# The norm inside the layers, applied by GpSimd instead of ScalarE, in a macaron block of attention, experts and a recurrence

## The chip, the cores and the metric

One core of a Trainium2 chip runs the whole kernel. The metric is the time of one execution on the device, in microseconds. The kernel before took 5356.07 us in the median of three runs (5350.53, 5356.07, 5367.39).

## The reference, cut to what matters

The input is a batch of 8 sequences of 512 tokens with 128 features. Six blocks follow each other; the change touches the second, a stack of six layers:

```
for l in range(LAYERS):                      # 6
    keys = concatenate([past, x])            # past: one row of zeros
    q, k, v = x @ Wq.T + bq, keys @ Wk.T + bk, keys @ Wv.T + bv     # 16 heads of 8
    scores = q @ k.T / sqrt(8), only keys at 0 to 125 places before the query
    o = softmax(scores) @ v;  o = o @ Wo[l].T + bo[l]
    x = _ln(x + o, ln1_g[l], ln1_b[l])       # norm of kind 1
    ff = gelu(x @ W1[l].T + b1[l]) @ W2[l].T + b2[l]
    x = _ln(x + ff, ln2_g[l], ln2_b[l])      # norm of kind 2
# _ln(x, g, b) = (x - mean) * rsqrt(var + 1e-5) * g + b, over the 128 features
```

Ahead of the layers stands a block of routed experts, behind them another one, then causal attention with a mixture of experts, a recurrence over time, and attention with experts again.

## The kernel before, in words

The activations of all tokens lie in `A`, 32 tiles of 128 tokens x 128 features, four tiles to a sequence. Each engine has its own program of the layers; they are tied together by semaphores, and each engine works strictly in the order in which its program is written.

**Stages, units, items.** A stage is one sequence in one layer: 6 x 8 = 48 stages. A stage is two units (r = 0 and 1), each with half of the heads, and a unit is four items (i = 0 to 3), one for each block of 128 keys. An item has two halves. In each half TensorE runs a `bracket`: scores of an item five ahead (`S`, L1251, read by VectorE for the row minima, L2197), and the turned scores of this item (`T`, L1266), which ScalarE turns into probabilities (L1832). GpSimd then masks the probabilities of an item by two `affine_select` (L945, L950), and TensorE multiplies them by the values (`values`, L1306) two items later: the values of item 0 stand in the program at item 2. The result banks are two rings: D, four banks that VectorE frees (`l_d_ev`), and A, three banks that ScalarE frees (`l_a_ev`).

**What runs beside it.** Projections of the next stage, the transposes and the feed-forward of earlier stages are put between the brackets (`shared`, `feed_forward`): in stage s, the projection of the heads' output of stage s - 1, the feed-forward's up part of stage s - 2 (L1227, six and two matmuls) and its down part of stage s - 3 (L1237). The norm of kind 1 of stage s - 2 belongs to unit 0 of stage s, the norm of kind 2 of stage s - 3 to unit 1. After the 48 stages three more empty out the pipeline, in which there is no attention.

**The norm.** VectorE adds the branch to `A` and takes mean and variance of each token (L2130, L2134) into `mv`, and signals `l_var_ready`. The rest was split over two engines:
- GpSimd, `root` (L954): at the start of a unit, ahead of the select of item 0, it takes the root of the variance by three Newton steps on 128 x 4 numbers (`newton_rows`, L910 to L928, each step linked to the one before by a semaphore), then multiplies the mean by it (L960) and negates the product (L961), into `r1`, and signals `l_rstd_ready`.
- ScalarE, `apply` (L1846): in the second item, after the exponentials of its first half, it waits for that signal, and for each of the four tiles computes `A * rstd + r1` in place (L1850), then signals `l_applied`. In its program the copy of the head sums (`sums`, L1844) and the exponentials of the item's second half come next.
- GpSimd, `affine` (L963): after the select of item 1 it waits for `l_applied` and multiplies by g (L970) and adds b (L971) over all four tiles, and signals the turned rows of the next step (`attn_out`, `ffn_out`). The results of kind 1 are wanted in unit 1 of the same stage, those of kind 2 by the next layer.

`chain.link` waits for the instruction that it issues, `chain.add` only counts it, and `chain.join` waits for all that were counted.

Of the kernel before, what the change touches and what calls it, by code (L numbers as in the profile page):

```python
# [20 lines left out]
ALU = mybir.AluOpType  # L21
ACT = mybir.ActivationFunctionType
# [3 lines left out]
BATCHES, TOKENS = 8, 512  # L26
TPB = TOKENS // P
# [25 lines left out]
class Tally:  # L53


    def __init__(self):
        self.base, self.n = 0, 0
# [110 lines left out]
class LayerPipeline:  # L168
# [9 lines left out]
    def __init__(self, sem):  # L178
        both = (0, 1)
        self.scored = [ScoreItem(0, both, 0, KPAD + P, True)] + \  # L180
            [ScoreItem(i, both, KPAD + P * (i - 1), 2 * P) for i in range(1, TPB)]
        self.turned = [TurnedItem(j, both, P * j, min(2 * P, TOKENS - P * j)) for j in range(TPB)]
        self.d_done, self.d_ev = sem("l_d_done"), sem("l_d_ev")
        self.a_done, self.a_ev = sem("l_a_done"), sem("l_a_ev")
        self.mask_done = sem("l_mask_done")
        self.pv_done = sem("l_pv_done")
        self.od_ev = sem("l_od_ev")
        self.pad_ready = sem("l_pad_ready")
        self.rows_ready = sem("l_rows_ready")
        self.var_ready = sem("l_var_ready")  # L190
        self.rstd_ready = sem("l_rstd_ready")
        self.applied = sem("l_applied")
        self.D, self.A, self.norm = {}, {}, {}
        self.number(("D", "prep", 0))
        for use in self.first_projections():
            self.number(use)
        for m in range(self.LEAD):
            for g in range(4):
                self.number(("D", "S", m, g))
        self.number(("D", "max0", 0))  # L200
        for u in range(self.UNITS + 5):
            for i in range(self.ITEMS):
                for half in range(2):
                    for use in self.bracket(u, i, half) + self.shared(u, i, half):
                        self.number(use)
            if u % 2:
                for use in self.feed_forward(u // 2):
                    self.number(use)
        for s in range(self.STAGES + 2):
            if 0 <= s - 1 < self.STAGES:  # L210
                self.norm[1, s - 1] = len(self.norm)
            if 0 <= s - 2 < self.STAGES:
                self.norm[2, s - 2] = len(self.norm)
# [217 lines left out]
def build(nc, d, out):  # L431
    ctx = ExitStack()
    with ctx:
        def sb(name, shape, dt=F32):
            return ctx.enter_context(nc.sbuf_tensor(name, shape, dt))
# [47 lines left out]
        r1 = sb("r1", [P, TILES])  # L483
        r2 = sb("r2", [P, TILES])
        stats = sb("stats", [P, TILES, 6])
        mv = sb("mv", [P, TILES, 2])
        rstd = sb("rstd", [P, TILES])
# [6 lines left out]
        at = [0]  # L494

        def take(*shape):
            n = int(np.prod(shape))
            v = arena[:, at[0]:at[0] + n]
            at[0] += n
            assert at[0] <= 34048  # L500
            if len(shape) == 2:
                v = v.rearrange("p (a b) -> p a b", b=shape[1])
            if len(shape) == 3:
                v = v.rearrange("p (a b c) -> p a b c", b=shape[1], c=shape[2])
            return v


        A = take(TILES, P)
# [115 lines left out]
        L = LayerPipeline(sem)  # L624
# [218 lines left out]
        def _(pool):  # L843
            chain = Chain(pool, g_chain)
# [44 lines left out]
            m = mask_win0[:, 1:2]  # L889
# [12 lines left out]
            m = mask_win0[:, KPAD:]  # L902
# [34 lines left out]
            def layers():  # L937

                def select(m):
                    t = L.turned[m % L.ITEMS]  # L940
                    view = PTs[m % L.SLOTS][:, 0:8 * t.w].rearrange("p (h q) -> p h q", q=t.w)

                    pool.wait_ge(L.a_ev, L.A["T", m, 3] + 1)
                    a = view[:, :, 0:P]
                    pool.affine_select(out=a, in_=a, compare_op=ALU.is_ge, fill=0.0, base=0,  # L945
                                       pattern=[[0, 8], [1, P]], channel_multiplier=-1).then_inc(L.mask_done, 1)

                    pool.wait_ge(L.mask_done, 2 * m + 1)
                    a = view[:, :, PAST + 1:t.w]
                    pool.affine_select(out=a, in_=a, compare_op=ALU.is_ge, fill=0.0, base=-1,  # L950
                                       pattern=[[0, 8], [-1, t.w - PAST - 1]], channel_multiplier=1)\
                        .then_inc(L.mask_done, 1)

                def root(kind, s):  # L954
                    at = TPB * (s % BATCHES)
                    n = L.norm[kind, s]
                    nb = r1[:, at:at + TPB]
                    pool.wait_ge(L.var_ready, n + 1)
                    chain.link(newton_rows(TPB, at))
                    chain.link(pool.tensor_tensor(nb, mv[:, at:at + TPB, 0], rstd[:, at:at + TPB], ALU.mult))  # L960
                    pool.tensor_scalar(nb, nb, -1.0, None, ALU.mult).then_inc(L.rstd_ready, 1)  # L961

                def affine(kind, s):  # L963
                    l, b = divmod(s, BATCHES)
                    x = A[:, TPB * b:TPB * (b + 1), :]
                    rows, g = (arows[l % 2], 2) if kind == 1 else (frows[l % 2], 1)
                    pool.wait_ge(L.applied, L.norm[kind, s] + 1)

                    pool.wait_ge(L.rows_ready, 2 * l + 1 if kind == 1 else min(2 * l + 2, 2 * LAYERS - 1))
                    chain.link(pool.tensor_tensor(x, x, row(rows[:, g, :]), ALU.mult))  # L970
                    pool.tensor_tensor(x, x, row(rows[:, g + 1, :]), ALU.add)\  # L971
                        .then_inc(attn_out if kind == 1 else ffn_out, 1)

                for s in range(L.STAGES + 3):
                    for r in range(2):
                        kind, b = (1, s - 2) if r == 0 else (2, s - 3)
                        normed = 0 <= b < L.STAGES
                        if normed:
                            root(kind, b)
                        for i in range(L.ITEMS):  # L980
                            if s < L.STAGES:
                                select(L.ITEMS * (2 * s + r) + i)
                            if i == 1 and normed:
                                affine(kind, b)
                            enter(0, s, r, i)
# [790 lines left out]
        def _(act):  # L1776
            chain = Chain(act, a_chain)
# [3 lines left out]
            def layers():  # L1781
# [61 lines left out]
                        act.wait_ge(L.d_done, L.D["od", u - 1] + 1)  # L1843
                    act.activation(ODs[0], ps[:, L.SUMS, :], copy).then_inc(L.od_ev, 1)  # L1844

                def apply(kind, s):  # L1846
                    act.wait_ge(L.rstd_ready, L.norm[kind, s] + 1)
                    for i in range(TPB):
                        t = TPB * (s % BATCHES) + i
                        m = act.activation(A[:, t, :], A[:, t, :], ACT.Identity, bias=r1[:, t:t + 1],  # L1850
                                           scale=rstd[:, t:t + 1])
                    m.then_inc(L.applied, 1)

                def shared(u, i, half):
                    for ring, name, n, *r in L.shared(u, i, half):
                        if ring == "D":
# [20 lines left out]
                for u in range(L.UNITS + 6):  # L1877
                    s, r = divmod(u, 2)
                    for i in range(L.ITEMS):
                        for half in range(2):  # L1880
                            if (i, half) == (1, 1) and 0 < u <= L.UNITS:
                                sums(u - 1)
                            if u < L.UNITS:
                                for k in (2 * half, 2 * half + 1):
                                    probs(L.ITEMS * u + i, k)
                            shared(u, i, half)
                            if (i, half) == (0, 1) and u + 1 < L.UNITS:
                                pad_probs(u + 1)
                            if (i, half) == (1, 0):
                                kind, b = (1, s - 2) if r == 0 else (2, s - 3)  # L1890
                                if 0 <= b < L.STAGES:
                                    apply(kind, b)
                    if r:
                        for ring, name, n, *c in L.feed_forward(s):
                            if ring == "A":
                                hidden(n, *c)
# [211 lines left out]
            for b in range(2, BATCHES):  # L2108
                act.wait_ge(R.y_done, b + 1)
                for i in range(TPB):  # L2110
                    t = TPB * b + i
                    m = act.activation(A[:, t, :], ps[:, 4 + b % 4, i * P:(i + 1) * P], ACT.Identity,
                                       bias=zero[:, 0:1], scale=rstd[:, t:t + 1])
# [708 lines left out]
```

## Time and profile before

| | |
|---|---|
| median of 3 runs | 5356.07 us |
| profiled execution, its own time | 5366.25 us |
| its span | 5364.5 us |
| TensorE busy (matmuls) | 4340.6 us, 81% |
| VectorE busy | 3354.4 us, 63% |
| ScalarE busy | 2537.7 us, 47% |
| GpSimd busy | 1798.7 us, 34% |
| mean granted clock of TensorE | 0.877 |
| ScalarE's applies (L1850) | 384 in the layers, 484 ns each |

The busy shares are means over blocks with different limits. The layers run from about 295 to 2420 us; of what follows, the change touches nothing. In the profile PE is TensorE's matmuls and PEld its weight loads, DVE is VectorE, ACT is ScalarE and POOL is GpSimd; L1850 is line 1850 of the kernel. A row with "x4" merges four instructions of one line that follow each other, with the time from the first's start to the last's end. What stands in brackets is the idle time of the engine ahead of the instruction, and what ended it. `arena` is the large buffer that holds nearly all tiles.

### The profile page before, as it was taken

How to read it: one execution, taken by the hardware profiler on the slowest of the kernel's cores; microseconds unless marked ns; L12 is line 12 of the kernel's file. 1: busy time of each engine (PE TensorE's matmuls, PEld its weight loads, DVE VectorE, ACT ScalarE, POOL GpSimd, SP SyncE). 2: the span in 40 equal slices, each digit the busy share in tenths (PEclk: the TensorE clock that was granted, in tenths of full speed). 3: DMA queues.
4: the chain of work that ended last, by engine and by line, in shares of the span. 5: the costliest groups of instructions: out<-in, count | busy, mean ns of one | idle time of the engine just before them, and what ended most of it. 6: DMA issues, size and time to landing. Idle time of an engine off the chain costs nothing.

```text
span 5364.5 us, 114679 instructions
## 1 busy us (share of the span) xinstructions
PE 4340.6 (81%) x42902; PEld 2557.6 (48%) x42902; DVE 3354.4 (63%) x15572; ACT 2537.7 (47%) x4908; POOL 1798.7 (34%) x3712
## 2 busy tenths in 40 slices
PE   2789999999999999972689999657470069999999
PEld 2645555555555555542643446435340034446777
DVE  2187777777777777732156752699999957772111
ACT  1346777777777777741334544333230024553333
POOL 3155666666666666653123220000000022220000
PEclk9879999999999999985878989778685558998999
DMA  4500000000000000002401000010000000000000
GB/s 125 153 10 2 2 12 2 6 8 2 12 2 6 8 2 6 2 1 79 142 5 39 1 1 13 13 25 16 16 17 16 0 11 1 1 1 3 5 5 7
DMA packets 131690, 104.40 MB, mean 19 GB/s; under 512 B 22048, under 2 KB 110400, under 8 KB 131136
## 3 DMA queue, kind: packets, MB, share of 16 engines
q1 hardware_dynamic: 127040, 88.67, 6.1%
q0 software_dynamic: 4096, 8.40, 0.5%
q8 instruction: 341, 5.59, 0.4%
q14 instruction: 213, 1.74, 0.1%
HBM read 74.56 MB, written 22.48 MB: 18 GB/s over the span
## 4 chain that ended last, share of the span: by engine, by line
PE 58%; DVE 21%; ACT 7%; POOL 7%; issue 6%; SPq 1%; DMA 1%; POOLq 0%; DVEq 0%; ACTq 0%
PE ps L1676 6%; PE ps L1668 6%; PE ps L1266 5%; PE ps L1306 5%; PE ps L1451 4%; PE ps L1251 4%; PE ps L1463 4%; PE ps L1227 3%; PE ps L1237 3%; PE ps L1492 2%; DVE arena L2697 2%; DVE arena L2717 2%; PE ps L1136 2%; ACT arena L1850 2%; ACT arena L1832 2%
## 5 line engine op out<-in xcount | busy, mean ns | idle before, releaser
L2197 DVE CUSTOM_DVE_ANT_0 arena<-ps,mask_win 128x256 f32<-128x256 f32 (+1 forms) x3072 | 1008.6, 385 | 257.1 <-PE ps L1251 255.1
L1832 ACT ACTIVATE arena<-ps 128x512 f32<-128x512 f32 (+1 forms) x1536 | 751.5, 543 | 562.6 <-PE ps L1266 553.9
L1266 PE MATMUL ps<-arena 32*64 32x384 f32 (+2 forms) x6144 | 742.9, 478 | 72.6 <-ACT arena L1832 72.2
L1676 PEld LDWEIGHTS ps<-w,arena 128*128 128x128 f32 x4096 | 546.8, 196 | 356.9 <-issue 282.1
L1251 PE MATMUL ps<-arena 32*64 32x192 f32 (+2 forms) x12288 | 694.6, 323 | 14.7 <-DVE arena L2197 14.1
L1676 PE MATMUL ps<-w,arena 128*128 128x128 f32 x4096 | 554.5, 279 | 115.5 <-ACT arena L2086 63.1
L2086 ACT ACTIVATE arena<-ps,eb 128x512 f32<-128x512 f32 x512 | 351.1, 687 | 621.6 <-PE ps L1668 621.4
L2370 DVE CUSTOM_DVE_ANT_0 arena<-ps,mask_cau 128x512 f32<-128x512 f32 (+3 forms) x1024 | 446.4, 486 | 272.7 <-PE ps L1451 270.2
L1949 ACT ACTIVATE arena<-ps 128x512 f32<-128x512 f32 (+2 forms) x768 | 363.0, 526 | 482.9 <-PE ps L1463 482.8
L945 POOL TENSOR_SCALAR_AFFINE_SELECT arena<-arena 128x1024 f32<-128x1024 f32 x384 | 419.8, 1093 | 394.2 <-ACT arena L1832 391.4
L1668 PE MATMUL ps<-arena,w 128*128 128x512 f32 x1024 | 537.0, 608 | 0.0
L1463 PE MATMUL ps<-arena 32*128 32x512 f32 (+2 forms) x1536 | 503.0, 643 | 24.2 <-ACT arena L1949 24.0
L1251 PEld LDWEIGHTS ps<-arena 32*64 32x64 f32 x12288 | 379.9, 133 | 270.5 <-DVE arena L2197 96.0
L1451 PE MATMUL ps<-arena 32*128 32x512 f32 (+3 forms) x2048 | 437.3, 529 | 22.4 <-DVE arena L2370 17.1
L2598 DVE SCALAR_TENSOR_TENSOR X<-ps,C,X 128x128 f32<-128x128 f32 x512 | 143.7, 343 | 469.0 <-PE ps L1676 468.9
L1306 PE MATMUL ps<-arena 128*32 128x256 f32 (+1 forms) x6144 | 387.4, 371 | 14.1 <-POOL arena L950 14.1
L997 POOL TENSOR_SCALAR_AFFINE_SELECT arena<-arena 128x512 f32<-128x512 f32 (+1 forms) x192 | 153.6, 801 | 727.8 <-ACT arena L1949 727.2
L1136 PE MATMUL ps<-ident,arena 128*128 128x128 f32 x912 | 170.2, 318 | 271.4 <-DMA arena<-xs 120.5
L950 POOL TENSOR_SCALAR_AFFINE_SELECT arena<-arena 128x1040 f32<-128x1040 f32 (+1 forms) x384 | 341.8, 890 | 26.2
L910 POOL TENSOR_SCALAR nv<-mv 128x4 f32<-128x4 f32 (+3 forms) x136 | 32.1, 236 | 855.5 <-DVE mv L2134 850.9
L1451 PEld LDWEIGHTS ps<-arena 32*128 32x128 f32 x2048 | 198.1, 212 | 190.6 <-issue 90.2
L1266 PEld LDWEIGHTS ps<-arena 32*64 32x64 f32 x6144 | 217.5, 132 | 149.5 <-ACT arena L1832 145.8
(315 smaller groups left out, 7683.4 us busy)
## 6 DMA issues: line engine op xcount, KB each, us to landing
w<-in_L_w_dram SPq DMA_DIRECT2D x160, 256.0 KB
arena<-xs SPq DMA_DIRECT2D x10, 512.0 KB, 6.8
ys<-arena SPq DMA_DIRECT2D x10, 512.0 KB, 4.4
xs<-zero SPq DMA_DIRECT2D x1, 2560.0 KB, 11.2
w<-in_L_w_dram SPq DMA_DIRECT2D x1, 2048.0 KB
scr_k<-arena SPq DMA_DIRECT2D x8, 256.0 KB, 2.3
scr_v<-arena SPq DMA_DIRECT2D x8, 256.0 KB, 2.8
scr_f<-arena SPq DMA_DIRECT2D x8, 256.0 KB, 3.2
```

The source lines that it names most:

```text
L945: pool.affine_select(out=a, in_=a, compare_op=ALU.is_ge, fill=0.0, base=0, pattern=[[0, 8], [1, P]], channel_multiplier=-1).then_inc(L.mas ...
L1251: m = pe.matmul(ps[64 * h:64 * h + 64, bank, s.at(v) + lo:s.at(v) + hi], Q[p][r][rows, v, q0:q0 + 64], K[p][r][rows, s.k0 + lo:s.k0 + hi], ...
L1266: m = pe.matmul(out[64 * h:64 * h + 64, :, lo:hi], K[p][r][rows, t.k0 + lo:t.k0 + lo + 64], Q[p][r][rows, 0:2, t.q0 + lo:t.q0 + hi], start ...
L1306: x = pe.matmul(ps[32 * g:32 * g + 32, L.SUMS, t.q0:t.q0 + t.w], Vx[p][:, t.block, at:at + 32], PTs[m % L.SLOTS][:, (2 * k + v) * t.w:(2 * ...
L1451: m = pe.matmul(ps[:, g, s.at(v):s.at(v) + s.kw], Q[p][r][rows, v, s.tile * P:(s.tile + 1) * P], K[p][r][rows, s.k0:s.k0 + s.kw], start=Tr ...
L1463: pe.matmul(ps[:, 4 + k % 2, 0:w].rearrange("p (v q) -> p v q", q=t.w), K[p][r][rows, t.k0:t.k0 + P], Q[p][r][rows, t.vs[0]:t.vs[-1] + 1, ...
L1668: pe.matmul(out if use else out.rearrange("p (i t) -> p i t", t=P), E1(e)[:, c * P:(c + 1) * P], rows(g), start=True, stop=True).then_inc( ...
L1676: m = pe.matmul(ps[:, 2 + e % 2, i * P:(i + 1) * P], hid[c % 2][:, i * P:(i + 1) * P], E2(e)[:, c, :], start=(c == 0 and i == 0), stop=(c ...
L1832: act.activation(PTs[m % L.SLOTS][:, k * w:(k + 1) * w], bank[:, 0:w], exp, scale=-1.0)\
L1949: act.activation(PT[i % 2][:, k * w:(k + 1) * w], ps[:, 4 + k % 2, 0:w], exp, scale=-1.0)\
L2197: x = dve.tensor_tensor_reduce(out=seen, in0=bank[:, s.at(v):s.at(v) + s.kw], in1=mask, scale=1.0, scalar=NO_SCORE, op0=ALU.add, op1=ALU.m ...
L2370: m = dve.tensor_tensor_reduce(out=junk[:, g, s.at(v):s.at(v) + s.kw], in0=ps[:, g, s.at(v):s.at(v) + s.kw], in1=mask, scale=1.0, scalar=N ...
```

## The change

GpSimd no longer makes the product of mean and root, and no longer hands over. Right after the root it applies the norm itself, one `tensor_scalar` a tile (subtract the mean, multiply by the root, both read as columns), ahead of the select of item 0. `affine` waits for GpSimd's own four instructions instead of ScalarE's. ScalarE's `apply` and its call go, with the two semaphores.

```
                 def root(kind, s):
                     at = TPB * (s % BATCHES)
                     n = L.norm[kind, s]
-                    nb = r1[:, at:at + TPB]
                     pool.wait_ge(L.var_ready, n + 1)
                     chain.link(newton_rows(TPB, at))
-                    chain.link(pool.tensor_tensor(nb, mv[:, at:at + TPB, 0], rstd[:, at:at + TPB], ALU.mult))
-                    pool.tensor_scalar(nb, nb, -1.0, None, ALU.mult).then_inc(L.rstd_ready, 1)
+                    for t in range(at, at + TPB):
+                        chain.add(pool.tensor_scalar(A[:, t, :], A[:, t, :], mv[:, t, 0:1], rstd[:, t:t + 1],
+                                                     ALU.subtract, ALU.mult))
...
-                    pool.wait_ge(L.applied, L.norm[kind, s] + 1)
-
+                    chain.join()
...
-                def apply(kind, s):
-                    act.wait_ge(L.rstd_ready, L.norm[kind, s] + 1)
-                    for i in range(TPB):
-                        t = TPB * (s % BATCHES) + i
-                        m = act.activation(A[:, t, :], A[:, t, :], ACT.Identity, bias=r1[:, t:t + 1],
-                                           scale=rstd[:, t:t + 1])
-                    m.then_inc(L.applied, 1)
...
-                            if (i, half) == (1, 0):
-                                kind, b = (1, s - 2) if r == 0 else (2, s - 3)
-                                if 0 <= b < L.STAGES:
-                                    apply(kind, b)
```

## Rows read from the trace of the kernel before

**Rows 1.** The page's first line.

```profile
span 5364.5 us, 114679 instructions
```

**Rows 2.** Busy time in a stretch: length, each engine's busy us, clock.

```profile
400.00:2300.00 1900.00, 1824.29 (x26878) 1024.32 (x26876) 1404.49 (x7308) 1372.47 (x2684) 1209.18 (x2328) 0.99 0.02 5
```

**Rows 3.** Waits, 400 to 2300 us: total, times, longest.

```profile
PEld ps L1266 <- ACT arena L1832: 136.8, 219, 1.7
...
PE ps L1266 <- ACT arena L1832: 67.9, 88, 1.3
...
ACT arena L1850 <- POOL r L961: 15.4, 44, 0.6
```

**Rows 4.** The chain that ended last, 400 to 2300 us, then one stage: start, us.

```profile
by line: PE ps L1266 12.1%; PE ps L1306 11.9%; PE ps L1251 11.3%; PE ps L1227 8.4%; PE ps L1237 8.3%; issue 7.8%; ACT arena L1832 5.7%; ACT arena L1850 5.5%; PE ps L1180 5.0%; PE ps L1202 3.0%; POOL arena L945 2.6%; PE ps L1195 2.5%; PE ps 
...
1003.69 1.53 ACT arena L1850 x4
...
1014.56 1.10 POOL arena L945
```

**Rows 5.** The same chain's first and last L1227 x6 of 44.

```profile
437.38 2.68 PE ps L1227 x6
...
2264.59 2.78 PE ps L1227 x6
```

**Rows 6.** Busy time in two microseconds of a long period, clock third last.

```profile
982.00:984.00 2.00, 2.00 (x16) 0.93 (x8) 0.91 (x6) 0.00 (x0) 1.99 (x2) 0.50 0.00 0
```

**Rows 7.** Timeline of TensorE, one stage.

```profile
1005.10 0.59 PE L1251 MATMUL ps<-arena 32*64 32x192 f32 x8
1006.24 1.02 PE L1266 MATMUL ps<-arena 32*64 32x384 f32 x6 [0.54 <-ACT arena L1832]
...
1007.51 1.07 PE L1306 MATMUL ps<-arena 128*32 128x256 f32 x16
...
1022.09 0.56 PE L1251 MATMUL ps<-arena 32*64 32x192 f32 x8
1023.62 1.02 PE L1266 MATMUL ps<-arena 32*64 32x384 f32 x6 [0.98 <-ACT arena L1832]
...
1024.90 1.07 PE L1306 MATMUL ps<-arena 128*32 128x256 f32 x16
...
1026.48 0.39 PE L1251 MATMUL ps<-arena 32*64 32x192 f32 x4
...
1027.32 0.66 PE L1136 MATMUL ps<-ident,arena 128*128 128x128 f32 x4
```

**Rows 8.** Timeline of VectorE, the same stage.

```profile
1007.69 0.42 DVE L2197 CUSTOM_DVE_ANT_0 arena<-ps,mask_win 128x256 f32<-128x256 f32 x1 [1.21 <-PE ps L1251]
```

**Rows 9.** Timeline of GpSimd, the same stage.

```profile
1001.26 1.10 POOL L950 TENSOR_SCALAR_AFFINE_SELECT arena<-arena 128x1040 f32<-128x1040 f32 x1
...
1020.42 0.20 POOL L960 TENSOR_TENSOR r<-mv,rstd 128x4 f32<-128x4 f32 x1
1020.70 0.23 POOL L961 TENSOR_SCALAR r<-r 128x4 f32<-128x4 f32 x1
1020.88 1.10 POOL L945 TENSOR_SCALAR_AFFINE_SELECT arena<-arena 128x1024 f32<-128x1024 f32 x1
1022.05 1.10 POOL L950 TENSOR_SCALAR_AFFINE_SELECT arena<-arena 128x1040 f32<-128x1040 f32 x1
```

**Rows 10.** Groups by line and shape on GpSimd: busy us, mean ns.

```profile
L970 POOL TENSOR_TENSOR arena<-arena 128x512 f32<-128x512 f32 x48 | 60.9, 1269 | 8.8 <-ACT arena L1850 8.8
...
L2767 POOL TENSOR_TENSOR frow<-frow 128x128 f32<-128x128 f32 x12 | 6.0, 503 | 0.9
...
L2768 POOL TENSOR_SCALAR frow<-frow 128x128 f32<-128x128 f32 x12 | 3.6, 300 | 1.1
```

**Rows 11.** Timeline of GpSimd, in the tail.

```profile
2417.00 0.20 POOL L960 TENSOR_TENSOR r<-mv,rstd 128x4 f32<-128x4 f32 x1
...
2419.28 1.26 POOL L970 TENSOR_TENSOR arena<-arena 128x512 f32<-128x512 f32 x1 [1.76 <-ACT arena L1850]
```

More of the change, by code:

```diff
@@ L190, in __init__ @@
         self.var_ready = sem("l_var_ready")
-        self.rstd_ready = sem("l_rstd_ready")
-        self.applied = sem("l_applied")
         self.D, self.A, self.norm = {}, {}, {}
```

## The prediction, made before the changed kernel was run

> **What bounds the kernel now.** The change touches the stretch in which the six layers run. The span is 5364.5 us [rows 1]; the layers' steady part, 400 to 2300 us, has TensorE busy for 1824 of 1900 us at a granted clock of 0.99, with GpSimd at 1209 and ScalarE at 1372 [rows 2]. I read first who waits for whom there. TensorE's stops are mostly for ScalarE's exponentials (L1832): 136.8 us of weight loads and 67.9 us of matmuls, and ScalarE in turn waits for the roots' last instruction (L961) 44 times, 15.4 us [rows 3]. Then the chain that ended last: the norm's apply on ScalarE (L1850) is 5.5% of those 1900 us, about 104 us, the largest share of a line that the change removes; two pieces of it in one stage show where [rows 4]. Last, the period: from the first to the last "L1227 x6" of the chain are 43 periods in 1827.2 us, 42.5 us each [rows 5]; 32 of them take about 42.05 us, 11 take 1.4 to 2.4 us more, 17.5 us together. In such a long one the clock stood at 0.50, the lower of the two levels (1.2 GHz), from 982 us on [rows 6], about 2 us after TensorE had stood still for ScalarE.
>
> A stage is two units of four items. One stage in TensorE's timeline [rows 7]: in both units the fault is at the same place, the bracket of item 2. In the first unit it starts with scores at 1005.10, its turned scores wait until 1006.24 for a bank that ScalarE frees after its four applies, and the values of item 0 (L1306) follow at 1007.51. In the second unit: 1022.09, 1023.62, 1024.90. The same bracket one place later, where nothing is waited for, takes from 1026.48 to 1027.32, 0.84 us. So the applies hold TensorE back for 1007.51 - 1005.94 = 1.57 us in the first unit and for 1024.90 - 1022.93 = 1.97 us in the second. VectorE doesn't hold the place: it stood idle 1.21 us before 1007.69, waiting for these scores [rows 8].
>
> **What goes.** 96 times four ACTIVATEs on ScalarE, with a wait for GpSimd ahead of them; the chain charges 1.53 us to those at 1003.69 [rows 4]. Nothing takes their place on ScalarE, which goes straight to the copy of the sums and the next exponentials. The copy needs the values of item 3, which TensorE issues ahead of the scores of 1005.10, so it isn't late. On GpSimd the product (L960) and the negation (L961) go: from L960's start at 1020.42 to the select at 1020.88 are 0.46 us [rows 9].
>
> **What comes.** 96 times four tensor_scalar (128x128, two column operands) on GpSimd, ahead of the select of item 0, with the affine's wait turned into a wait for GpSimd's own results. No row shows this form. Nearest is the tensor_scalar 128x128 with constants: 300 ns; the two-input tensor_tensor 128x128 takes 503 ns [rows 10]. An instruction of GpSimd that waits for no result starts some 0.05 us before the end of the last (the select at 1020.88 after L961, 1020.70 + 0.23 [rows 9]), so they start 0.25 to 0.50 us apart. I take 0.33, near the lower row, since the form also reads one tensor, with something added for reading the two columns: 4 x 0.33 = 1.32 us, net 1.32 - 0.46 = 0.86 us more on GpSimd before each select of item 0.
>
> The Trainium skill (GPSIMD Engine Reference, section 3.1, "Elementwise") speaks against this move: its best case is about 1.8 cycles an element, an estimate of 192 ns for 128 elements at the 1.2 GHz it divides by, beside whatever an instruction costs at least. By that rule the four would be nearer to 0.39 us each than to 0.33, and the second unit's gain 0.24 us smaller, 11 us in all; the row of 300 ns speaks for less.
>
> Who waits behind the four: select 0, then select 1, the affine, selects 2 and 3, all in this order on GpSimd; behind select 0, the values of item 0 on TensorE.
> - First unit: select 0 ends at 1001.26 + 1.10 = 1002.36 [rows 9], later 1003.22. TensorE will want it at 1005.94. 2.7 us of cover, so the 0.86 us costs nothing, and the 1.57 us is gained but for a hand-off: I take 1.5. GpSimd's later selects wait for exponentials that come earlier by as much.
> - Second unit: GpSimd works without a pause from the select of item 3 (1014.56, [rows 4]) through the root to select 0, whose end is 1022.05 + 1.10 = 1023.15 [rows 9]. With 0.86 us added and 0.10 for the hand-off (estimate), the values of item 0 can start at 1024.11, where TensorE would be ready at 1022.93. **The next thing late is GpSimd.** Gain 1024.90 - 1024.11 = 0.79 us rather than 1.97. With 0.50 us an instruction it is 1024.79, gain 0.11; with 0.25 it is 1023.79, gain 1.11.
> - The affine's results are wanted much later than they are made (8 stages on, or in the next unit), and GpSimd's load of 1209 us in 1900 grows by 88 x 0.86 = 76 us: no bound by sum.
>
> **Tail.** When attention has ended, five applies lie bare on the chain: L960 starts at 2417.00, the affine at 2419.28, 2.28 us [rows 11]. It becomes 1.32 + 0.1 = 1.42; I take 0.8 us each.
>
> **Sum.** First units with both norm and attention: 46, 46 x 1.5 = 69. Second units: 45 x 0.79 = 36. Tail 5 x 0.8 = 4. Together 109 us. The profiled execution took 5366.25 us (span 5364.5), so 5257 for such a one; the median of the runs was 5356.07, 10 us below it, hence 5247. I give 5250, a few us back for stages that differ from the one read.
>
> Bounds: GpSimd's price moves the second units between 5 and 50 us. The first units give at least what TensorE shows as its own idle time at that place (0.54 us, [rows 7]), 25 us, and at most 1.57, 72 us. So the gain is 34 to 126 us, and 17 more if the long periods vanish.
>
> **Rivals.**
> - *Only the marked idle time comes back*: TensorE's weight loads and VectorE's score minima take over right behind the gap. For it: VectorE was at work until 1007.69 - 1.21 = 1006.48, after the turned scores had started. Against: the 1.21 us of idle time themselves, in which it waited for these very scores [rows 8]. Gain 46 x 0.54 + 45 x 0.79 + 4 = 64 us: 5292.
> - *The clock*: a full stop of TensorE before the second unit's values stays (1022.93 to 1024.11, 1.18 us, against 0.98 now). The clock fell after such a stop in 11 of 43 periods, 1.6 us each [rows 5, 6]. If it fell in all 45, 34 more falls cost 54 us: 5301. Against: the stop is hardly longer, and the first unit's vanishes; the falls may as well get fewer, down to 5230. The Trainium skill (TensorE: Matmul & The Clock Gate, Part 1) has the clock set by how busy the engine has lately been; by that rule either way is open.
> - *The column form is slow on GpSimd*, and the time is lost at one place, the select of item 0 in the second unit. At q us an instruction the values start at 1022.79 + 4q, a loss of 4q - 2.11 against now; with the first unit's 1.5 us kept, gain and loss cancel at 45 (4q - 2.11) + 5 (4q - 2.18) = 69, q = 0.87 us. Above it the kernel is slower. If each of the four cost what a whole 128x512 tensor_tensor does, 1.27 us [rows 10], the second units lose 2.97 us each, the first still gain 0.43, the tail loses 2.9 each: 134 - 20 + 15 = 129 us, 5485. For it: no row shows columns read by GpSimd. Against: 0.87 is nearly three times the row of the same shape.
> - *The change does nothing of note*: only at q near 0.87, so it is the middle of the last one.
>
> **Chances.** Forecast (second unit held by GpSimd, about 5250): 0.62. Marked idle only, 5292: 0.18. Clock, 5301: 0.06. Slow columns: 0.14, of which 0.05 lies near 0.87 us and 0.09 above. A difference of 0.3% (16 us) is about what a measurement of this kernel can tell from none. Faster 0.62 + 0.18 + 0.06 = 0.86, same 0.05, slower 0.09. The range takes in the first three cases and the bounds of the unknown price: 5215 (no falls of the clock, cheap columns) to 5325 (gain 34 us, rounded up); what is left out is the slow columns and some 0.06 beside the ends.
>
> **What would show it.** Right: the period falls from 42.05 to about 39.8 us; ScalarE has no gap of L1850 before the sums; the first unit's bracket of item 2 takes under 1 us; in the second unit L1306 waits for GpSimd's select (L950 in today's numbers) instead of turned scores for ScalarE, about a microsecond 45 times; the new instructions start 0.3 to 0.4 us apart. Wrong: the new instructions start over 0.5 us apart; the wait for ScalarE stays in the first unit; TensorE's weight loads wait for VectorE for much longer than now; more than 20 periods with the clock at its lower level.

## The result, and the profile after

The changed kernel took 5363.5 us in the median of 13 runs (5359.13 to 5373.52), the kernel before 5353.92 in 13 runs beside it; the ratio is 1.0018, 95% interval 1.0011 to 1.0025. The forecast was 5250, range 5215 to 5325. So nothing of the 109 us came. The change loses 10 us, 0.18%: less than the 0.3% that the prediction took for no change.

First the page of the changed kernel: the span, the busy time by engine, and the group of the new instructions (line 958; count, busy us, mean ns, idle time before). Lines stand 2 or 3 lower than before in the first two thirds of the code: L1248 scores, L1263 turned scores, L1303 values, L943 and L948 the select.

```profile
span 5365.6 us, 114487 instructions
...
PE 4289.4 (80%) x42902; PEld 2569.0 (48%) x42902; DVE 3352.4 (62%) x15572; ACT 2404.0 (45%) x4524; POOL 2055.5 (38%) x3904
...
L958 POOL TENSOR_SCALAR arena<-arena,mv,rstd 128x128 f32<-128x128 f32 x384 | 300.8, 796 | 10.5
```

ScalarE's busy time fell by 134 us and GpSimd's grew by 257 us: 384 instructions of **796 ns**, where the forecast took 0.33 us from start to start. The same stretch as [rows 2], 400 to 2300 us:

```profile
400.00:2300.00 1900.00, 1770.12 (x26503) 1028.61 (x26495) 1380.28 (x7202) 1234.20 (x2299) 1424.69 (x2471) 0.95 0.02 5
```

TensorE is busy for 54 us less, at a granted clock of 0.95 in place of 0.99. And this is who waits for whom there (total, times, longest), beside [rows 3]:

```profile
PEld ps L1303 <- POOL arena L948: 146.6, 45, 4.4
PE ps L1303 <- POOL arena L948: 125.0, 44, 3.9
...
PEld ps L1263 <- ACT arena L1829: 5.6, 19, 0.3
```

The wait of the turned scores for ScalarE is gone, 136.8 to 5.6 us. In its place the values wait for GpSimd's select, 44 times 2.8 us. One stage on TensorE, to be laid beside [rows 7]:

```profile
1011.79 0.43 PE L1248 MATMUL ps<-arena 32*64 32x192 f32 x4
...
1012.70 1.07 PE L1303 MATMUL ps<-arena 128*32 128x256 f32 x16
...
1027.27 0.39 PE L1248 MATMUL ps<-arena 32*64 32x192 f32 x4
...
1031.06 1.94 PE L1303 MATMUL ps<-arena 128*32 128x256 f32 x16 [2.80 <-POOL arena L948]
```

In unit 0 the bracket of item 2 now takes 1012.70 - 1011.79 = 0.91 us to the values, where it took 2.41. In unit 1 it is through at once too, and then TensorE stands still for 2.80 us. GpSimd in that unit, beside [rows 9]:

```profile
1025.65 3.13 POOL L958 TENSOR_SCALAR arena<-arena,mv,rstd 128x128 f32<-128x128 f32 x4
1028.74 1.10 POOL L943 TENSOR_SCALAR_AFFINE_SELECT arena<-arena 128x1024 f32<-128x1024 f32 x1
1029.90 1.10 POOL L948 TENSOR_SCALAR_AFFINE_SELECT arena<-arena 128x1040 f32<-128x1040 f32 x1
```

The four take 3.09 us until the select starts, the second select ends at 1031.00, and the values start at 1031.06. Those 16 matmuls take 1.94 us where they took 1.07. TensorE's busy time and granted clock (third number from the end) in two-microsecond steps show why:

```profile
1026.00:1028.00 2.00, 2.00 (x44) 1.00 0.04 8
1028.00:1030.00 2.00, 0.27 (x8) 1.00 0.00 0
1030.00:1032.00 2.00, 0.94 (x12) 0.54 0.00 0
...
1034.00:1036.00 2.00, 2.00 (x28) 0.50 0.00 0
...
1038.00:1040.00 2.00, 2.00 (x40) 1.00 0.00 0
```

During the stop the clock falls to its lower level of 1.2 GHz, and here it stays there for 6.8 us, longer than behind most others. I counted such falls by the same view in steps of 1 us from 440 to 2140 us: **10 before, 39 after**, with 34 and 153 us at the lower level. One of the 39 is under way at 440 us, ahead of the first of these stops. The period (first L1211, the heads' projection, of a stage to the next) went from 42.05 to 42.86 us in the median, from 42.49 to 42.94 in the mean of 44.

### The profile page after: what moved, and what is told of

The parts are those of the page before. It is cut to its first block, busy times and chain, and to the rows that moved or that the text cites. A ratio compares the mean times of both kernels' runs of the same rounds, so it can differ in the third digit from the quotient of the medians.

```text
span 5365.6 us, 114487 instructions
## 1 busy us (share of the span) xinstructions
PE 4289.4 (80%) x42902; PEld 2569.0 (48%) x42902; DVE 3352.4 (62%) x15572; ACT 2404.0 (45%) x4524; POOL 2055.5 (38%) x3904
## 4 chain that ended last, share of the span: by engine, by line
PE 58%; DVE 21%; POOL 12%; issue 4%; ACT 3%; DMA 1%; SPq 0%; POOLq 0%; DVEq 0%; ACTq 0%
PE ps L1673 6%; PE ps L1665 6%; PE ps L1303 5%; PE ps L1248 5%; PE ps L1448 4%; PE ps L1460 4%; PE ps L1224 3%; PE ps L1234 3%; POOL arena L958 3%; PE ps L1263 3%; PE ps L1177 3%; PE ps L1133 2%; PE ps L1489 2%; DVE arena L2682 2%; DVE arena L2702 2%
## 5 line engine op out<-in xcount | busy, mean ns | idle before, releaser
L1263 PE MATMUL ps<-arena 32*64 32x384 f32 (+2 forms) x6144 | 711.7, 487 | 1.3 <-ACT arena L1829 0.8
L1248 PE MATMUL ps<-arena 32*64 32x192 f32 (+2 forms) x12288 | 684.3, 328 | 14.4 <-DVE arena L2182 13.8
L1248 PEld LDWEIGHTS ps<-arena 32*64 32x64 f32 x12288 | 397.6, 137 | 281.6 <-DVE arena L2182 95.7
L1303 PE MATMUL ps<-arena 128*32 128x256 f32 (+1 forms) x6144 | 400.0, 381 | 147.0 <-POOL arena L948 147.0
L943 POOL TENSOR_SCALAR_AFFINE_SELECT arena<-arena 128x1024 f32<-128x1024 f32 x384 | 419.9, 1093 | 171.4 <-ACT arena L1829 170.7
L948 POOL TENSOR_SCALAR_AFFINE_SELECT arena<-arena 128x1040 f32<-128x1040 f32 (+1 forms) x384 | 341.8, 890 | 26.2
L1303 PEld LDWEIGHTS ps<-arena 128*32 128x32 f32 x6144 | 162.3, 113 | 353.3 <-POOL arena L948 174.1
L958 POOL TENSOR_SCALAR arena<-arena,mv,rstd 128x128 f32<-128x128 f32 x384 | 300.8, 796 | 10.5
```

The source lines that it names most:

```text
L958: chain.add(pool.tensor_scalar(A[:, t, :], A[:, t, :], mv[:, t, 0:1], rstd[:, t:t + 1], ALU.subtract, ALU.mult))
L1248: m = pe.matmul(ps[64 * h:64 * h + 64, bank, s.at(v) + lo:s.at(v) + hi], Q[p][r][rows, v, q0:q0 + 64], K[p][r][rows, s.k0 + lo:s.k0 + hi], ...
L1263: m = pe.matmul(out[64 * h:64 * h + 64, :, lo:hi], K[p][r][rows, t.k0 + lo:t.k0 + lo + 64], Q[p][r][rows, 0:2, t.q0 + lo:t.q0 + hi], start ...
L1303: x = pe.matmul(ps[32 * g:32 * g + 32, L.SUMS, t.q0:t.q0 + t.w], Vx[p][:, t.block, at:at + 32], PTs[m % L.SLOTS][:, (2 * k + v) * t.w:(2 * ...
```

## The experiments

All ran beside the kernel before. "Stop" is the idle time that TensorE shows in unit 1 of a stage near 1000 to 1045 us, ahead of the turned scores of item 2 where ScalarE holds it (before, e1) and ahead of the values of item 0 in the others. "Falls" are those from 440 to 2140 us; in all but before, e2, e7 and e10 one of them is the fall under way at 440 us, so the 1 of e4, e5, e9 and e11 means none behind a stop in unit 1. "Each" is the duration of one of the new instructions. e3 leaves the norm of the layers out and e7 alters it; they serve for their times alone.

| kernel | median us | ratio to before, 95% | period us | stop us | falls | each ns |
|---|---|---|---|---|---|---|
| before | 5353.9 | 1 | 42.05 | 0.98 | 10 | none |
| changed | 5363.5 | 1.0011 to 1.0025 | 42.86 | 2.80 | 39 | 796 |
| e1 kind 1 only | 5302.6 | 0.9889 to 0.9928 | 40.59 | 1.02 | 11 | 800 |
| e2 kind 2 only | 5435.2 | 1.0141 to 1.0178 | 44.39 | 2.82 | 33 | 799 |
| e3 constants | 5279.4 | 0.9840 to 0.9881 | 40.84 | 2.11 | 8 | 645 |
| e4 kind 2 later | **5172.6** | 0.9652 to 0.9691 | 38.66 | none | 1 | 796 |
| e5 kept busy, six | 5410.3 | 1.0077 to 1.0130 | 44.01 | none | 1 | 800 |
| e11 kept busy, three | 5301.6 | 0.9885 to 0.9926 | 41.53 | none | 1 | 796 |
| e7 one column | 5323.1, one run | | 42.48 | 2.51 | 30 | 717, 719 |
| e8 multiply, add | 5277.5 | 0.9825 to 0.9875 | 40.76 | 2.08 | 4 | 456 |
| e6 two wide | 5279.7 | 0.9838 to 0.9878 | 40.51 | 1.78 | 11 | 1043, 1040 |
| e10 ScalarE later | 5275.2 | 0.9824 to 0.9871 | 40.81 | 1.48 | 0 | none |
| e9 later, multiply, add | 5184.7 | 0.9666 to 0.9699 | 39.01 | 0.28 | 1 | 453 |

**e1 and e2: the two halves of the change.** `root` of one kind ends as in the kernel before, and ScalarE's `apply` and the wait for it stay for that kind alone.

```
                     chain.link(newton_rows(TPB, at))
+                    if kind == 2:        # e2: kind == 1
+                        ... product, negation, rstd_ready, as before
+                        return
                     for t in range(at, at + TPB):
```

> GpSimd applies the norm of kind 1 (unit 0 of a stage) alone; the norm of kind 2 stays with ScalarE as before. Theory: the change gains 1.57 us a stage in unit 0, where GpSimd has 2.7 us to spare, and loses about 1.0 us in unit 1, where the four instructions of 0.77 us stand ahead of a select that TensorE waits for, and about 1.4 us more because the long stop drops TensorE's clock. Then this half alone gains 46 x 1.5 = 70 us: about 5285, a period near 40.5 us, and no more falls of the clock than the 12 of before. Rival (the new instructions cost something wherever they stand, by GpSimd's load or by the memory port it shares with VectorE): half of the change's loss, within 10 us of 5355.

> The other half: GpSimd applies the norm of kind 2 (unit 1) alone, ScalarE that of kind 1. Theory: unit 0 keeps its hold, unit 1 loses 1.0 us a stage to GpSimd, and the stop drops the clock in nearly every stage: 45 x 1.0 + 32 more falls x 1.5 = 93 us slower, about 5445, period near 44.3. Rival as above: within 10 us of 5355. Rival (falls of the clock come and go by themselves): 5400, with some 12 falls.

Turned scores of unit 1 in e1 (L1273), values of unit 1 in e2 (L1313), on TensorE:

```profile
1005.28 1.02 PE L1273 MATMUL ps<-arena 32*64 32x384 f32 x6 [1.02 <-ACT arena L1839]
```

```profile
1005.69 1.93 PE L1313 MATMUL ps<-arena 128*32 128x256 f32 x16 [2.82 <-POOL arena L950]
...
1030.40 1.03 PE L1273 MATMUL ps<-arena 32*64 32x384 f32 x6 [0.54 <-ACT arena L1839]
```

The two halves pull in opposite directions. With unit 0 alone changed (e1) the period is 42.05 - 40.59 = 1.46 us shorter, with the new instructions at 800 ns as in the other runs; with unit 1 alone (e2) it is 2.34 longer, with 33 falls of the clock, and 5435 us were measured for the 5445 expected. The rival that the instructions cost something wherever they stand has fallen. (Its "memory port" is a rule of the Trainium skill, SBUF — State Buffer, section "Who interferes with whom": a VectorE instruction with two inputs in SBUF contends with a GpSimd instruction that reads there. No run here shows it for these four: in the changed kernel their shortest is 788 ns and their median 793, and from 2300 us on, where the pipeline empties and VectorE has less to do, the median is 792.) In time, e1 came 18 us short of 5285: its 44 periods give 1.43 us each in the mean, 63 us, its profiled execution took 65 us less than that of before, and its timed runs 50 less. What took the difference is open.

**e4: kind 2 applied later.** This is the fastest version.

```
                     chain.link(newton_rows(TPB, at))
-                    for t in range(at, at + TPB):
-                        chain.add(pool.tensor_scalar(...))
+                    if kind == 1:
+                        apply(at)            # the same four instructions
...
+                    if kind == 2:
+                        apply(TPB * b)       # in affine, behind the select of item 1
                     chain.join()
```

> The changed kernel with the four instructions of kind 2 moved from ahead of the select of item 0 to behind the select of item 1, ahead of the affine; kind 1 stays ahead of item 0. Theory: both units gain what ScalarE's applies cost, 1.57 + 1.97 us a stage, GpSimd is in time for every select, no stop is left and the clock stays up: 45 x 3.5 + 17 = 175 us faster, about 5180 to 5200, period 38.5, under 5 falls. Rival (GpSimd's later selects then come late, as it works 75% of the time): the stop moves to the values of item 2 or 3 and 5250 to 5300 is measured.

GpSimd in unit 1 of one stage (L962 the four, L973 the affine), and the whole stretch of 440 to 2140 us (busy time of PE, PEld, DVE, ACT, POOL, then the clock):

```profile
1011.76 1.10 POOL L943 TENSOR_SCALAR_AFFINE_SELECT arena<-arena 128x1024 f32<-128x1024 f32 x1
...
1015.15 1.10 POOL L948 TENSOR_SCALAR_AFFINE_SELECT arena<-arena 128x1040 f32<-128x1040 f32 x1
1016.24 3.13 POOL L962 TENSOR_SCALAR arena<-arena,mv,rstd 128x128 f32<-128x128 f32 x4
1019.46 1.27 POOL L973 TENSOR_TENSOR arena<-arena 128x512 f32<-128x512 f32 x1
```

```profile
440.00:2140.00 1700.00, 1700.00 (x26524) 994.83 (x26522) 1350.00 (x7176) 1231.50 (x2301) 1422.99 (x2456) 1.00 0.02 6
```

TensorE shows no idle time in 1700 us, the clock is at 1.00, and GpSimd's 84% does no harm. The same instructions at the same 796 ns cost 191 us more when those of kind 2 stand ahead of the select of item 0 instead of behind that of item 1; the falls of the clock are part of that.

**e5 and e11: is it the stop that drops the clock?** Extra matmuls in unit 1 ahead of the wait for the select; the second run has three in place of six. In both, the wait for `L.od_ev`, which stood behind that for the select, stands ahead of the new lines.

```
+                    if m % L.ITEMS == 0 and u % 2:
+                        for _ in range(6):   # e11: 3
+                            pe.matmul(ps[:, L.SUMS, :], ident[:], pos.rearrange("p i f -> p (i f)"),
+                                      start=True, stop=True, skip_group_check=True)
                     pe.wait_ge(L.mask_done, 2 * m + 2)
```

> The changed kernel with six more 128x512 matmuls on TensorE in unit 1, ahead of the wait for the select of item 0, so that it works while it waits (their results are overwritten). Theory: the stop itself drops the clock, and a dropped clock costs about 1.4 us of the 42.86 us period; kept busy, the clock stays up and 45 x 1.4 = 60 us come back: about 5300, period 41.5, under 15 falls in 440 to 2140 us, where the changed kernel has 39. Rival (the falls have another cause, as the higher share of work in unit 0): 39 falls as now and 5360 or more.

> As the run e5_kept_busy, with three extra matmuls in place of six, as each is issued twice and takes 0.44 us an issue: 2.65 us of work in the 2.8 us stop, so that they hold nothing up. Theory: the clock stays up and the period is 41.5 us, which is 42.86 less the 1.4 us of a fallen clock: 45 x 1.4 = 60 us under the changed kernel, 5295 to 5310, under 5 falls in 440 to 2140 us. Rival (the clock is not what the period's last 1.4 us are): period 42.8 and 5355 with the clock up.

The extra matmuls in e5 and in e11 (L1298), in e11 with the values behind them (L1307):

```profile
1044.60 5.42 PE L1298 MATMUL ps<-pos,ident 128*128 128x512 f32 x12
```

```profile
1012.40 2.84 PE L1298 MATMUL ps<-pos,ident 128*128 128x512 f32 x6
1015.28 1.07 PE L1307 MATMUL ps<-arena 128*32 128x256 f32 x16
```

And the stretch of 440 to 2140 us of e11:

```profile
440.00:2140.00 1700.00, 1698.12 (x24929) 970.23 (x24929) 1269.56 (x6683) 1147.57 (x2144) 1325.91 (x2290) 1.00 0.02 6
```

Six statements are twelve rows and 5.42 us, twice the stop: they put off the values themselves, so e5's time missed the expected 5300 and is no test, though the falls that are gone are one. With the right amount, e11, **useless work makes the changed kernel 62 us faster**: the falls go from 39 to 1 and the period from 42.86 to 41.53. The values of item 0 still wait for the same select: it ends at 1015.22 (1014.12 + 1.10 on GpSimd), they start at 1015.28, and they take 1.07 us in place of 1.94. So a fallen clock costs 1.33 us a period, and the stop causes it. The periods of single runs say the same. In the changed kernel the one period without a fall takes 41.53 us, the 32 with one 42.85 in the median and the 6 with two 43.7. In e7, 10 without take 41.23 and 29 with one 42.60. In the kernel before, e1 and e6 a fall costs 1.5 to 1.6 us.

**e3, e7, e8, e6: what the four instructions cost.** The operands and operations were varied; e8 also makes `r1` again ahead of them, 0.46 us, and e6 has two wide instructions in place of four.

```
-  A[:, t, :], A[:, t, :], mv[:, t, 0:1], rstd[:, t:t + 1], ALU.subtract, ALU.mult    # changed
+  A[:, t, :], A[:, t, :], 0.25, 0.5,                       ALU.subtract, ALU.mult    # e3
+  A[:, t, :], A[:, t, :], mv[:, t, 0:1], 2.0               ALU.subtract, ALU.mult    # e7, kind 1
+  A[:, t, :], A[:, t, :], 0.5, rstd[:, t:t + 1],           ALU.subtract, ALU.mult    # e7, kind 2
+  A[:, t, :], A[:, t, :], rstd[:, t:t + 1], r1[:, t:t + 1], ALU.mult, ALU.add        # e8, r1 as before
+  x = A[:, at:at + TPB, :]                                                           # e6: two in all, shortened
+  tensor_tensor(x, x, mean spread, ALU.subtract); tensor_tensor(x, x, root spread, ALU.mult)
```

> The changed kernel with two constants instead of the two columns in the four instructions (the layers' norm is left out by it, its root is still computed). Theory: the price of the columns alone made the forecast wrong; with constants they start about 0.27 us apart, L303's stop in unit 1 is about 1.1 us and the time is that of the forecast, 5235 to 5260, with 10 to 20 falls of the clock. Rival (the place in the order or the sharing with VectorE is what costs): the instructions stay near 0.8 us or the time stays above 5320.

> The changed kernel with one column and one constant in the four instructions: mean column and a constant factor for kind 1, a constant and the root column for kind 2 (the layers' norm is changed by it). For their durations alone. Theory: each column adds about 0.075 us to the 0.645 of the form with constants, so 0.72 us in both kinds. Rival (the first column turns on a slower path): 0.79 in both.

> The changed kernel with another pair of operations: GpSimd makes minus mean times root as before (0.46 us) and the four instructions multiply by one column and add the other, where the change subtracts and multiplies. With constants, subtract and multiply took 0.645 us in the run before this one, and multiply and add 0.300 in the kernel before. Theory: the pair of operations is the larger part of the price, two columns add 0.15 us: 0.45 us each, the values of item 0 in unit 1 start where ScalarE let them start before, unit 0 keeps its 1.5 us: 5275 to 5290, period 40.5. Rival (every two-operation form in the layers costs 0.65 and more, because VectorE works beside it): 0.80 us each, period over 43, about 5385.

> The changed kernel with two tensor_tensor 128x512 (minus the mean, times the root, both spread over the columns) in place of the four tensor_scalar: 2.61 us in place of 3.09. Theory: the values of item 0 in unit 1 start 0.48 us earlier, a stop of 2.3 us. If the clock then falls as seldom as at the stop of 2.1 us (8 times in 440 to 2140 us), period 41.0 to 41.3 and about 5290; if it falls as at 2.8 us (39 times), 42.4 and 5345. Rival (a spread column costs a wide tensor_tensor more than the 1.27 us of the affine's): over 5365.

Groups of GpSimd by line and shape between 295 and 2420 us, of e3, e7, e8 and e6 in this order:

```profile
L958 POOL TENSOR_SCALAR arena<-arena 128x128 f32<-128x128 f32 x384 | 237.7, 645 | 8.4
```

```profile
L959 POOL TENSOR_SCALAR arena<-arena,rstd 128x128 f32<-128x128 f32 x192 | 135.9, 719 | 5.6
L959 POOL TENSOR_SCALAR arena<-arena,mv 128x128 f32<-128x128 f32 x192 | 135.0, 717 | 5.5
```

```profile
L961 POOL TENSOR_SCALAR arena<-arena,rstd,r 128x128 f32<-128x128 f32 x384 | 168.8, 456 | 10.0
```

```profile
L958 POOL TENSOR_TENSOR arena<-arena,mv 128x512 f32<-128x512 f32 x96 | 100.1, 1043 | 7.5
L960 POOL TENSOR_TENSOR arena<-arena,rstd 128x512 f32<-128x512 f32 x96 | 99.8, 1040 | 7.5
```

These are a ladder: subtract and multiply by constants takes 645 ns, with one column 717 or 719, with two 796, so 75 ns a column. Multiply and add with two columns 456, where the kernel before has 300 with constants [rows 10]. **The pair of operations makes 340 ns of it, the two columns 150.** My theory for e3 (the columns alone) was wrong, and its expected 0.27 us missed; so was e8's rival, that all two-operation forms are slow in the layers. e8 came where it was expected, within 5275 to 5290. e6 beat both its cases, with 11 falls: four columns, each spread over the 128 elements of its tile, make a tensor_tensor cheaper, 1040 ns against 1269 for the affine's with a spread row, not dearer.

Which pairs are dear, the kernel before showed already, in short rows. L910 only adds, L925 multiplies and adds, both with constants:

```profile
L925 POOL TENSOR_SCALAR nt<-nt 128x4 f32<-128x4 f32 x360 | 70.7, 196 | 71.2 <-POOL nt L922 71.2
...
L910 POOL TENSOR_SCALAR nv<-mv 128x4 f32<-128x4 f32 x120 | 28.0, 233 | 829.0 <-DVE mv L2134 825.0
...
L925 POOL TENSOR_SCALAR nt<-nt 128x32 f32<-128x32 f32 x6 | 1.3, 220 | 1.2 <-POOL nt L922 1.2
...
L910 POOL TENSOR_SCALAR nv<-mv 128x32 f32<-128x32 f32 x2 | 0.6, 312 | 17.7 <-DVE mv L2134 17.7
```

Twenty-eight more elements cost multiply and add 24 ns, 0.86 ns an element, and carried on to 128 that gives 302 ns, where 300 were read. The single addition grows by 79 ns, 2.8 an element, which carried on to 128 gives 583 ns (an estimate from rows with few counts; L925 at 24 elements, three times, lies off the line at 244), near the 645 of subtract and multiply. So of the forms seen here multiply and add is the cheap exception, and the forecast leant on its row.

**e10: the place on ScalarE.** The kernel before, with `apply` called at (2, 0) in place of (1, 0) and `affine` behind the select of item 2 in place of 1.

> The kernel before with ScalarE's four applies moved one item later, from item 1 to behind the first exponentials of item 2, and GpSimd's affine from behind the select of item 1 to behind that of item 2. Nothing changes its engine. Theory: what the applies cost is their place, ahead of the sums and the exponentials that free the banks for item 2; one item later ScalarE has 1.1 us (unit 0) and 1.8 us (unit 1) of idle time ahead of its next exponentials, so 1.0 and 1.7 us come back: 45 x 2.7 = 120 us, about 5235. Rival (ScalarE's 1.65 us is paid wherever it stands): within 20 us of 5350.

The values of unit 1 on TensorE (L1306), and GpSimd from the affine of unit 0 on:

```profile
1003.95 1.07 PE L1306 MATMUL ps<-arena 128*32 128x256 f32 x16 [1.48 <-POOL arena L950]
```

```profile
994.07 1.28 POOL L971 TENSOR_TENSOR arena<-arena 128x512 f32<-128x512 f32 x1
995.30 1.09 POOL L945 TENSOR_SCALAR_AFFINE_SELECT arena<-arena 128x1024 f32<-128x1024 f32 x1
...
1001.62 1.10 POOL L945 TENSOR_SCALAR_AFFINE_SELECT arena<-arena 128x1024 f32<-128x1024 f32 x1
```

It gained half of what was expected: 1.24 us a period in place of 2.7. Still, without any change of engine, 78 us come from the place alone; some 16 of them are the ten falls of the clock that are gone. What took the rest is in these rows: the affine, put off with the apply, now stands ahead of the select of item 3 (995.30, with no wait before it), so root and select 0 of unit 1 start late, and TensorE waits 1.48 us for GpSimd.

**e9: both remedies.** `apply` as in e4, form and `r1` as in e8.

> The two remedies together: kind 2 applied behind the select of item 1 (as e4_second_later, 5172.6 us) in the form multiply and add (0.456 us for 0.796). Theory: behind the select of item 1 the price is hidden already, TensorE is without a stop, so the period stays at 38.66; only the emptying of the pipeline gains, 5 x (3.09 - 1.70 - 0.57) = 4 us: 5165 to 5173. Rival (GpSimd's load still holds something): 5150 or less.

```profile
1021.45 1.07 PE L1312 MATMUL ps<-arena 128*32 128x256 f32 x16 [0.28 <-POOL arena L948]
```

The period is 39.01 us, not the theory's 38.66, and the time lies above the expected 5165 to 5173: product and negation are back ahead of the select of item 0, and TensorE waits 0.28 us for it. The dear form at a hidden place is no worse than the cheap form with a preparation at the bare one; e4 and e9 can't be told apart by their intervals.

## Why the prediction was wrong

- **Where ScalarE held TensorE: right.** Unit 0 was to give 1.5 us; e1 gave 1.46 a period. All of the hold is gone when GpSimd is in time (e4): 42.05 - 38.66 = 3.39 us, against 1.57 + 1.97 = 3.54 read from two brackets.
- **That GpSimd would be late in unit 1: right**, and so was the rule for it. The prediction put the start of the values at 1022.79 + 4q. With the measured q of 3.09 / 4 = 0.77 that is a loss of 0.98 us against before; e11, which has the clock up, shows 41.53 - (42.05 - 1.46) = 0.94.
- **The price of the four instructions: the step that failed.** "I take 0.33, near the lower row, since the form also reads one tensor, with something added for reading the two columns." It was 0.77, outside of the 0.25 to 0.50 that stood as bounds. The row that it leant on, 300 ns, has other operations (multiply and add), and that was the larger part, by e3 and e8. The bounds were rows of the same shape, not of the same operations, and the two columns cost 0.15 us, where 0.33 leaves 0.08 over the 0.25 of the lower row. It cost 4 x 0.44 = 1.76 us a stage, 79 us in 45 stages. The Trainium skill (GPSIMD Engine Reference, section 3.1), weighed there with an estimate of 0.39 us each, pointed the right way and was half of what the runs show.
- **The clock: a rival that came true, sized well** (1.6 us a fall foreseen, 1.33 measured), but given 0.06, and tied to a stop of 1.18 us. At the stop of 2.80 it fell in nearly every stage: mean period 42.94 against 41.59 in e11, 59 us in 44 periods, of which the kernel before had already lost 17.5. Less those and with the 79 us above that makes 121 us. In the 44 periods the forecast was a gain of some 105 us and the result a loss of 44 x (42.94 - 42.49) = 20, a gap of 125. The gap in the whole time is 109 + 10 = 119; that it lies still closer to 121 is luck, since the emptying of the pipeline, below, is in the one and not in the other.
- **The rivals were kept apart.** "Slow columns" alone were to break even at 0.87 us; 0.77 would have left some 20 us of gain. A slower instruction makes a longer stop, and a stop of this length drops the clock: the two rivals are one chain, and the break-even is lower than either says.
- "Marked idle time only" is refuted by e1: 1.46 us came back where 0.54 was marked.
- **The emptying of the pipeline** was priced by the bare apply alone. That did lose, as a price of 0.77 has it: from the first of the four to the affine are 3.22 us (2427.54 to 2430.76), where it took 2.28. Yet the last two periods together took 62.96 us against 72.24. The rows show two differences the other way, which the sum didn't have, and no run takes them apart. In the last but one the clock of the kernel before stood at its lower level for 20.5 us, that of the changed kernel for 6.8. In the last, the feed-forward's up part waited in the kernel before for a copy (L1820) that stands behind `apply` in ScalarE's order, and `apply` for GpSimd's root; without `apply` the copy comes at once:

```profile
2376.88 4.78 PE L1227 MATMUL ps<-arena 128*128 128x512 f32 x6 [5.17 <-ACT arena L1820]
```

```profile
2390.34 5.37 PE L1224 MATMUL ps<-arena 128*128 128x512 f32 x6 [0.87 <-ACT arena L1817]
```

## What to carry to other kernels

Before work is moved to an engine with idle time, ask what stands right behind it in that engine's order: the same 3.1 us cost 191 us more ahead of the select that TensorE waited for than behind the next one. Take an instruction's price from a row with the same operations and operands, not only the same shape; where there is none, compare rows of two lengths for each kind of operation, as above, or let the bounds reach to twice the dearest near row. And price a stop of TensorE with the clock that it may cost behind it: here 1.3 to 1.6 us a fall, in nearly every stage with a stop of 2.8 us.

## What the runs showed of the hardware

- On GpSimd, tensor_scalar of 128x128 f32: multiply and add 300 ns (constants) and 456 (two columns); subtract and multiply 645, 718, 796 with none, one, two columns. From 4 to 32 elements, multiply and add grows by 0.86 ns an element (196 to 220 ns), a single addition by 2.8 (233 to 312).
- tensor_tensor of 128x512 f32 on GpSimd: 1269 ns with a row spread over the four tiles, 1040 with a column spread over 128.
- TensorE's clock against its stops in unit 1, some 40 of each in 440 to 2140 us, without the fall that is under way at 440: at 2.80 and 2.82 us of stop 38 and 33 falls, at 2.51 30, at 2.11 7, at 2.08 3, at 1.78 10, at 1.48 none, at 1.02 and 0.98 10 and 10, with 0.28 or none 0. So a stop of 2.5 us and more drops it mostly, one of 1 to 2.1 us in a quarter of the stages or fewer, and not in order of length; what decides there, no run shows. In the kernel before all ten fell behind the stop of about 1 us in unit 1 and none behind that of 0.54 in unit 0.
- Three extra matmuls that fill such a stop take 62 us off the time.
